# A decoder's sparse experts on one core: a gather waits for the fourth block ahead of it to be turned, in place of the eighth

## Chip, cores and metric

The kernel is one program on one NeuronCore of a Trainium2 chip. TensorE is PE in the views (its weight loads are PEld), VectorE is DVE, ScalarE is ACT, GpSimd is POOL, SyncE is SP. The metric is device time in microseconds, from start to end of one execution; lower is better. All times below are in microseconds unless they say ns.

## What is computed

Twelve sublayers (attention, cross attention and a feed-forward part in each of four layers) run over 1024 tokens of 256 features, each with a residual and a layer norm. The change lies in the last of them, a feed-forward part with 64 experts of which each token uses 8:

```python
logits = x.astype(jnp.float32) @ gate_weight.astype(jnp.float32).T
scores = jax.nn.softmax(logits, axis=-1)
topk_w, topk_idx = jax.lax.top_k(scores, K)          # K = 8 of E = 64
topk_w = topk_w / jnp.sum(topk_w, axis=-1, keepdims=True)
flat_ids = topk_idx.reshape(-1)
sorted_tokens = jnp.repeat(x, K, axis=0)[order]      # order = argsort(flat_ids)
g = jax.lax.ragged_dot(sorted_tokens, w_gate, group_sizes)
u = jax.lax.ragged_dot(sorted_tokens, w_up, group_sizes)
out = jax.lax.ragged_dot(jax.nn.silu(g) * u, w_down, group_sizes)
y = jnp.sum(out[inv].reshape(-1, K, h) * topk_w[:, :, None], axis=1)
```

Each expert has w_gate and w_up of 256x96 and w_down of 96x256. Everything is float32 here.

## The kernel before

The sublayer is `l3_ffn`. A first part (`l3f_route`) sorts the 8192 pairs of token and expert into 127 blocks of 128 places, each block belonging to one expert, and leaves `token_ids` (which token stands in each place) and `experts_row` (which expert each block has). The token rows lie in HBM as `moe_rows`.

The second part (`l3f_experts`) runs over the 127 blocks. Every engine has its own instruction stream, written out by hand, and they meet at semaphores:

- **POOL** (L2544) issues for block b one indirect DMA that gathers 128 rows of 1 KB from `moe_rows` into `rows[:, b % 8, :]`. The buffer is a ring of eight, `x_ring`. Ahead of the gather it waits on `x_turned`, the count of blocks whose rows PE has turned.
- **SP** (L2558) loads the block's expert, 320 KB, into one of six buffers (`w_ring`), once the down product of six blocks earlier is done, and then (L2552) stores the result of that earlier block, 128 KB, to `moe_out`.
- **PE** has, per block, `turn(b)`: wait for the gather, then two transposes (L2571), whose last adds to `x_turned`; `gates(b)`: eight products (L2582), after a wait for the expert's weights; `down(b)`: two instructions in the trace for one product (L2591), after a wait for `h`. The order on PE is turn(b+2), gates(b+1), down(b), for b from 0 on; turn(0), turn(1), gates(0) stand in front.
- **DVE** copies the turned rows from PSUM (L2629) and multiplies silu by the up part (L2657). At block 8, and at blocks 20, 30, ... 90, it also computes a piece of the routing weights (L2634 to L2647).
- **ACT** computes silu (L2611) and copies the down product out of PSUM (L2618).

The wait in front of a gather and what follows it, as they stand in the kernel before:

```python
for b in range(blocks):
    if b >= x_ring:
        pool.wait_ge(x_turned, b - x_ring + 1)
```

The third part (`l3f_combine`) waits on POOL for every store to `moe_out`, gathers eight rows per token from it with 64 indirect DMAs into the same ring `rows`, and DVE sums them (L2679, L2696). It uses `x_ring` for its own waits.

Of the kernel before, what the change touches and what calls it, by code (L numbers as in the profile page):

```python
# [2376 lines left out]
def l3_ffn(k, w):  # L2377
# [6 lines left out]
    numbers, token_past, earlier = w("numbers"), w("token"), w("earlier")  # L2384
    token, past_end = token_past[:, :TILES], token_past[:, TILES:]
    F16 = mybir.dt.float16
    x_ring, w_ring, y_ring = 8, 6, 8
    with ExitStack() as ctx:
        sb = lambda name, shape, dt=F32: k.sb(ctx, "l3f_" + name, shape, dt)
        p, top, tmp = sb("p", [P, TILES, experts]), sb("top", [P, TILES, 8]), sb("tmp", [P, chosen, experts])  # L2390
# [33 lines left out]
        with nc.Block("l3f_route") as block_:  # L2424
# [107 lines left out]
        x_turned, x_copied, gates_done, silu_done, h_done, down_done, y_copied, weighed = (  # L2532
            k.sem("l3f_" + n) for n in names)
# [3 lines left out]
        with nc.Block("l3f_experts") as block_:  # L2537
            @block_.gpsimd
            def _(pool):
                pool.wait_ge(rows_stored, 16)  # L2540
                for b in range(blocks):
                    if b >= x_ring:
                        pool.wait_ge(x_turned, b - x_ring + 1)
                    nc.gpsimd.indirect_dma_start(  # L2544
                        rows[:, b % x_ring, :], None, k.moe_rows,
                        bass.IndirectOffsetOnAxis(token_ids[:, b:b + 1], 0)).then_inc(gathered[b % x_ring], 16)
# [293 lines left out]
```

## Time and profile before

| what | value |
|---|---|
| median of 3 runs | 1949.35 (1949.25 to 1951.55) |
| the profiled execution, its own time | 1946.63 |
| its span, first to last instruction | 1944.8 |
| mean granted TensorE clock | 0.845 of full |
| PE / DVE / ACT / POOL busy, share of the span | 78% / 60% / 43% / 28% |
| DMA moved | 126.19 MB, mean 65 GB/s |

The span is the time between the first and the last instruction of the profiled execution; 1.8 us of its own time lie outside of it. The shares are averages over twelve sublayers with different limits. The change touches the stretch from 1611 us, where the first gather of rows is issued, to about 1845 us, where the combining part starts. So that stretch is read by itself.

### The profile page before, as it was taken

Reading aid. Unit: us, or ns where it says so; the run is one execution under the profiler, and the core shown is the slowest. Engines: PE = TensorE matmul, PEld = TensorE weight load, DVE = VectorE, ACT = ScalarE, POOL = GpSimd, SP = SyncE. Lnnn points to the kernel's source line nnn. Section 1 sums busy time; section 2 is a strip of 40 time slices with the busy share of each in tenths; the row PEclk is TensorE's granted clock in tenths of the full one; section 3 lists DMA queues with packets and bytes.
Section 4 is the critical chain, followed back from the end, with each engine's and each line's share of the span. In section 5 each row is a group of like instructions: output and inputs, shape, how many; then the busy total and the mean of one; then the engine's idle time right before and its main releaser. Section 6 shows DMA issues by size and latency. Waiting matters only on the chain. (4 is left out here: it accounts for less than half of the span.)

```text
span 1944.8 us, 25982 instructions
## 1 busy us (share of the span) xinstructions
PE 1512.2 (78%) x8419; PEld 917.9 (47%) x8419; DVE 1166.2 (60%) x2266; ACT 839.7 (43%) x1649; POOL 554.0 (28%) x578
## 2 busy tenths in 40 slices
PE   5899879986268377768799997899899877999800
PEld 4746635555143122226344445434566456888700
DVE  3537742245755699997999995444366452444343
ACT  2337521122633665634799993211364232333300
POOL 0110100212110599964100001011300415555375
PEclk9999989998679699999655556999999978999955
DMA  2010000010100000001233332000000007999832
GB/s 85 10 61 2 2 22 0 25 57 6 44 30 0 0 1 0 1 1 78 39 74 74 72 71 55 0 1 0 1 2 1 16 22 231 342 347 340 288 108 86
DMA packets 117813, 126.19 MB, mean 65 GB/s; under 512 B 75088, under 2 KB 93648, under 8 KB 116272
## 3 DMA queue, kind: packets, MB, share of 16 engines
q1 hardware_dynamic: 108512, 99.48, 16.7%
q0 software_dynamic: 9168, 25.05, 4.1%
q8 instruction: 69, 1.13, 0.2%
q14 instruction: 64, 0.52, 0.1%
HBM read 88.97 MB, written 18.74 MB: 55 GB/s over the span
## 5 line engine op out<-in xcount | busy, mean ns | idle before, releaser
L446 POOL TENSOR_TENSOR rstd<-var,minus_half 128x1 f32<-128x1 f32 x96 | 61.2, 637 | 724.5 <-DVE var L430 724.5
L1672 POOL TENSOR_TENSOR l_drive<-l_area,l_xpad 128x512 f32<-128x512 f32 x128 | 158.4, 1270 | 88.8 <-ACT l_xpad L1690 88.8
L1646 PE MATMUL psum<-l_drive,consts 128*128 128x512 f32 x256 | 136.1, 635 | 37.8 <-DVE l_drive L1737 37.8
L2069 ACT ACTIVATE l2x_rings<-psum,l2x_mx,l2x_q_s 128x1024 f32<-128x1024 f32 x128 | 154.2, 1205 | 9.0 <-DVE l2x_mx L2040 6.8
L2544 POOL DMA_INDIRECT l3f_rows<-moe_rows,l3f_token_ids x127 | 120.5, 949 | 123.6 <-PE psum L2571 89.4
L2026 DVE TENSOR_REDUCE l2x_mx<-psum 128x1 f32<-128x1024 f32 x128 | 155.1, 1212 | 0.9 <-PE psum L1992 0.9
L1731 DVE TENSOR_TENSOR_SCAN l_state<-psum,l_drive 128x512 f32<-128x512 f32 x128 | 152.1, 1208 | 5.2 <-ACT psum L1703 4.5
L1992 PE MATMUL psum<-l2x_kT,l2x_qT 48*128 48x512 bf16 x256 | 129.9, 612 | 14.4 <-ACT l2x_rings L2069 6.2
L2582 PE MATMUL psum<-l3f_xT,l3f_of_expert 128*96 128x128 f32 x1016 | 134.1, 276 | 0.2
L2629 DVE COPY l3f_xT<-psum 128x256 f32<-128x256 f32 x127 | 53.9, 425 | 133.3 <-PE psum L2571 123.8
L363 ACT ACTIVATE XT<-psum 128x256 f32<-128x256 f32 x88 | 33.8, 384 | 220.1 <-PE psum L398 220.1
L2582 PEld LDWEIGHTS psum<-l3f_xT,l3f_of_expert 128*96 128x96 f32 x1016 | 119.9, 165 | 0.9 <-DMA l3f_of_expert<-in_experts 0.9
L951 DVE TENSOR_REDUCE mx<-psum 128x2 f32<-128x512 f32 (+1 forms) x128 | 79.0, 619 | 54.1 <-PE psum L883 53.5
L1703 ACT ACTIVATE psum<-l_area,l_a_neg 128x510 f32<-128x510 f32 x128 | 87.9, 688 | 46.0 <-DVE l_state L1731 45.7
L2591 PE MATMUL psum<-l3f_of_expert,l3f_h 96*128 96x256 f32 x254 | 88.5, 430 | 14.2 <-DVE l3f_h L2657 8.2
L1646 PEld LDWEIGHTS psum<-l_drive,consts 128*128 128x128 f32 x256 | 44.7, 195 | 104.9 <-DVE l_drive L1737 87.1
L2036 DVE TENSOR_SCALAR l2x_rings<-l2x_rings 128x1024 bf16<-128x1024 f32 x128 | 87.3, 683 | 0.6 <-ACT l2x_rings L2069 0.6
L424 DVE SCALAR_TENSOR_TENSOR R<-X,psum 128x256 f32<-128x256 f32 x80 | 32.7, 409 | 85.6 <-PE psum L387 85.6
L2611 ACT ACTIVATE l3f_silu<-psum 96x128 f32<-96x128 f32 x127 | 34.7, 273 | 103.2 <-PE psum L2582 83.1
L2002 PEld LDWEIGHTS psum<-identity_bf,l2x_rings 128*128 128x128 bf16 x512 | 49.5, 139 | 57.1 <-DVE l2x_rings L2036 57.1
L2679 POOL DMA_INDIRECT l3f_rows<-moe_out,l3f_place_ids x64 | 62.0, 968 | 37.3 <-DMA moe_out<-l3f_y_out 18.8
L2015 PEld LDWEIGHTS psum<-l2x_v,l2x_q_stack 128*128 128x128 bf16 x1024 | 44.9, 111 | 51.9 <-issue 51.0
(473 smaller groups left out, 3272.4 us busy)
## 6 DMA issues: line engine op xcount, KB each, us to landing
l3f_of_expert<-in_experts SPq DMA_DIRECT2D x127, 320.0 KB
moe_out<-l3f_y_out SPq DMA_DIRECT2D x127, 128.0 KB
arena<-in_pack SPq DMA_DIRECT2D x1, 3660.0 KB, 12.3
arena<-in_pack SPq DMA_DIRECT2D x1, 3277.0 KB, 10.3
arena<-in_pack SPq DMA_DIRECT2D x1, 2688.0 KB, 10.1
arena<-in_pack SPq DMA_DIRECT2D x1, 2303.0 KB, 9.0
l3f_rows<-moe_rows,l3f_token_ids POOLq DMA_INDIRECT x127
arena<-in_pack SPq DMA_DIRECT2D x1, 1538.0 KB, 6.7
```

The source lines that it names most:

```text
L951: nc.vector.tensor_reduce(mx[:, p % 4, :], two_heads(p), AX.X, ALU.max, negate=True)\
L1646: nc.tensor.matmul(sum_bank(c), k.identity[:, :], drive[:, (4 * i + c) % 8, :], start=n == 0, stop=n == states - 1, skip_group_check=True) ...
L1672: nc.gpsimd.tensor_tensor(drive[:, (4 * i + c) % 8, :], dx[:, c, half * HALF:(half + 1) * HALF], b_copy[:, i % 2, :], ALU.mult).then_inc(d ...
L1703: nc.scalar.activation(decay_bank(c).rearrange("p (b t) -> p b t", b=2)[:, :, 1:], source[:, :, 1:], ACT.Exp, scale=a_neg[:, c, n:n + 1]). ...
L1731: nc.vector.tensor_tensor_scan(state[:, c, :], decay_bank(c), drive[:, (4 * i + c) % 8, :], 0.0, ALU.mult, ALU.add).then_inc(scanned, 1)
L1992: last = nc.tensor.matmul(score_banks(i)[:, half, :], qT[rows, h // 2, tile * P:(tile + 1) * P], kT[rows, h // 2, half * HALF:(half + 1) * ...
L2026: nc.vector.tensor_reduce(mx[:, i % 4, 0:1], score_banks(i), AX.XY, ALU.max, negate=True).then_inc(max_taken, 1)
L2036: nc.vector.tensor_scalar(whole[:, u % 4, :], e[:, u % 3, :], ROUND, -ROUND, ALU.add, ALU.add).then_inc(rounded, 1)
L2069: nc.scalar.activation(e[:, i % 3, :], score_banks(i).rearrange("p b t -> p (b t)"), ACT.Exp, bias=mx[:, i % 4, 1:2], scale=q_s[:, i:i + 1 ...
L2544: nc.gpsimd.indirect_dma_start(rows[:, b % x_ring, :], None, k.moe_rows, bass.IndirectOffsetOnAxis(token_ids[:, b:b + 1], 0)).then_inc(gat ...
L2582: last = nc.tensor.matmul(k.bank(2 + b % 2)[:inter, n * P:(n + 1) * P], wgu[:, b % w_ring, c, n * inter:(n + 1) * inter], xT[:, b % 3, c, ...
L2591: nc.tensor.matmul(k.bank(4 + b % 2)[:, :D], h[:inter, b % 2, :], wd[:inter, b % w_ring, :], start=True, stop=True, skip_group_check=True) ...
```

## The change

The wait in front of the gather for block b asks for another count. Before, it was passed once PE had turned block b-8, which is also when the buffer that the gather writes comes free. Now it is passed once PE has turned block b-4. The ring keeps its eight buffers, and the gather still writes `rows[:, b % 8, :]`. Blocks 4 to 7 get a wait that they did not have. Nothing else differs; the combining part keeps its waits by `x_ring`.

```diff
-    x_ring, w_ring, y_ring = 8, 6, 8
+    x_ring, w_ring, y_ring, ahead = 8, 6, 8, 4
@@
                 for b in range(blocks):
-                    if b >= x_ring:
-                        pool.wait_ge(x_turned, b - x_ring + 1)
+                    if b >= ahead:
+                        pool.wait_ge(x_turned, b - ahead + 1)
                     nc.gpsimd.indirect_dma_start(
                         rows[:, b % x_ring, :], None, k.moe_rows,
                         bass.IndirectOffsetOnAxis(token_ids[:, b:b + 1], 0)).then_inc(gathered[b % x_ring], 16)
```

## Rows read from the trace of the kernel before

**Rows 1.** Busy time by stretch: us, engines, granted clock, DMA share, GB/s.
```profile
core 0: us, PE busy (x) PEld busy (x) DVE busy (x) ACT busy (x) POOL busy (x), PEclk, DMA share, GB/s
1611.00:1636.00 25.00, 15.37 (x88) 13.70 (x89) 4.54 (x14) 4.23 (x14) 15.40 (x16) 0.75 0.76 233
1636.00:1838.00 202.00, 192.87 (x1413) 173.44 (x1411) 90.56 (x264) 77.01 (x235) 105.06 (x111) 1.00 0.99 339
1838.00:1845.00 7.00, 4.61 (x28) 3.22 (x26) 1.18 (x4) 2.36 (x7) 0.00 (x0) 1.00 0.39 136
```

**Rows 2.** Waits, 1636 to 1838: who waits for whom, total us, times, longest.
```profile
POOL l3f_rows L2544 <- PE psum L2571: 85.9, 109, 2.2
...
PEld psum L2591 <- DVE l3f_h L2657: 9.9, 9, 1.4
...
PEld psum L2582 <- DMA l3f_of_expert<-in_experts: 0.4, 1, 0.4
```

**Rows 3.** Timeline of PE's weight loads: start, us, engine, line, operation.
```profile
1820.46 0.36 PEld L2571 LDWEIGHTS psum<-consts,l3f_rows 128*128 128x128 f32 x2
...
1822.09 0.36 PEld L2571 LDWEIGHTS psum<-consts,l3f_rows 128*128 128x128 f32 x2
...
1826.97 0.36 PEld L2571 LDWEIGHTS psum<-consts,l3f_rows 128*128 128x128 f32 x2
```

**Rows 4.** Timeline of POOL at the end of the blocks.
```profile
1821.34 0.94 POOL L2544 DMA_INDIRECT l3f_rows<-moe_rows,l3f_token_ids  x1 [0.69 <-PE psum L2571]
...
1826.22 0.94 POOL L2544 DMA_INDIRECT l3f_rows<-moe_rows,l3f_token_ids  x1 [0.68 <-PE psum L2571]
1845.91 0.94 POOL L2679 DMA_INDIRECT l3f_rows<-moe_out,l3f_place_ids  x1 [18.75 <-DMA moe_out<-l3f_y_out]
```

**Rows 5.** Timeline of the first gathers and of the first turn.
```profile
1610.96 1.22 POOL L2544 DMA_INDIRECT l3f_rows<-moe_rows,l3f_token_ids  x1 [27.92 <-POOLq L2424]
...
1612.48 0.95 POOL L2544 DMA_INDIRECT l3f_rows<-moe_rows,l3f_token_ids  x1 [0.30 <-issue]
...
1615.14 0.29 PEld L2571 LDWEIGHTS psum<-consts,l3f_rows 128*128 128x128 f32 x2 [6.42 <-DMA l3f_rows<-moe_rows,l3f_token_ids]
```

**Rows 6.** Timeline of POOL around one of DVE's extra pieces.
```profile
1662.01 0.95 POOL L2544 DMA_INDIRECT l3f_rows<-moe_rows,l3f_token_ids  x1 [0.68 <-PE psum L2571]
1664.71 0.95 POOL L2544 DMA_INDIRECT l3f_rows<-moe_rows,l3f_token_ids  x1 [1.75 <-PE psum L2571]
```

**Rows 7.** DMA queues, 1666.9 to 1667.2: packets, MB, share; q0 carries gathers.
```profile
q1 hardware_dynamic: 65, 0.12, 104.1%
q0 software_dynamic: 2, 0.00, 3.5%
```

**Rows 8.** DMA queues, 1667.2 to 1667.43, every queue that moved anything.
```profile
q1 hardware_dynamic: 52, 0.09, 97.5%
```

**Rows 9.** DMA queues, 1830 to 1830.5; in the next half microsecond q0 has none.
```profile
q1 hardware_dynamic: 110, 0.17, 94.3%
q0 software_dynamic: 5, 0.01, 4.3%
```

**Rows 10.** Timeline of PE near the start of the blocks.
```profile
1620.94 1.04 PE L2582 MATMUL psum<-l3f_xT,l3f_of_expert 128*96 128x128 f32 x8
1624.43 0.70 PE L2591 MATMUL psum<-l3f_of_expert,l3f_h 96*128 96x256 f32 x2 [2.45 <-issue]
...
1628.77 0.70 PE L2591 MATMUL psum<-l3f_of_expert,l3f_h 96*128 96x256 f32 x2 [2.55 <-issue]
```

**Rows 11.** The chain that ended last, 1830 to 1846: start, us, what.
```profile
1834.85 5.55 DMA l3f_of_expert<-in_experts
...
1840.44 1.13 PE psum L2582 x8
...
1843.38 1.68 DMA moe_out<-l3f_y_out
```

## The prediction, made before the changed kernel ran

> **What bounds the kernel now.** I read the busy time by stretch first, since the page's shares average over twelve sublayers. From 1636 to 1838 us PE is busy 192.87 of 202 us at the full granted clock (1.00, its 2.4 GHz level), and the DMA engines are busy for a share of 0.99 [rows 1]. So PE sets the pace and the transfers are nearly full beside it. The waits of the same stretch say who is late: POOL waits for PE 109 times in front of a gather, PE waits for DVE's `h` nine times (9.9 us), and PE waits for a DMA once, 0.4 us, for weights. It never waits for gathered rows there [rows 2]. Then the timeline gives the beat: turns begin at 1820.46, 1822.09 and, four blocks after the first, at 1826.97, so a block takes 6.51 / 4 = 1.63 us [rows 3]. POOL issues a gather 0.88 us after the start of the turn that releases it (1821.34 - 1820.46) [rows 3, 4].
>
> **What the change does to a gather.** The same turn still releases a gather, at the same place in the beat, but it is now the gather for the block four turns later. Before, it had eight blocks less 0.88 us, 13.01 - 0.88 = 12.1 us, to land. Now the gather issued at 1821.34 would be for the turn at 1826.97: 5.63 us [rows 3, 4]. No instruction is added in the steady part; the four new waits (blocks 4 to 7) are of a kind POOL passes 119 times already.
>
> What does a gather take, from its issue to its last packet, in this traffic? The gathers follow each other so closely on their queue (q0) that the last packet of one can be told only where a pause follows. The one issued at 1662.01 is followed by one at 1664.71 [rows 6]; q0 has two packets from 1666.9 to 1667.2 and none from there to 1667.43 [rows 7, 8]. So it ended 4.9 to 5.2 us after its issue. The last one, issued at 1826.22, has its last packets between 1830 and 1830.5, 3.8 to 4.3 us after [rows 4, 9]. The very first, beside the first loads of weights, was issued at 1610.96 and let PE start at 1615.14, 4.2 us [rows 5]. All three lie under 5.63 us, by 0.4 to 1.8 us. The typical gather is in time; the margin is thin, where before it was over 6.9 us.
>
> A rule speaks for a wider margin. The Trainium skill ("DMA: Bandwidth & Descriptors", Anatomy of one DMA) fits a DMA issued from GpSimd as about 2.0 us plus bytes over 436 GB/s. By that, an estimate for 128 KB is 2.3 us; no gather could be late, and the time would stay where it is. The rows above show 3.8 to 5.2 us at a DMA share of 0.99, so they decide here; the same page (Latency and other measured facts) says that HBM's latency is several times larger at high load, in which direction the trace agrees.
>
> **The price, part by part.**
>
> 1. Late gathers in the steady part. A turn that waits stops PE, and since PE sets the pace, the whole wait is lost: behind the turn on PE stand gates(b-1) and down(b-2), and behind them silu, `h`, the copy, the store and the next load. From below this costs 0, if the 111 gathers of the stretch behave like the three seen. From above: a large transfer in this traffic, a load of weights, took 5.55 us [rows 11]; no row shows one of a gather above 5.2. But 16 engines must finish for one gather, two of the three measured ones stood next to a pause or the end, and the three spread over more than a microsecond, so some of the 111 will pass 5.63. I take one in ten late by 0.2 us: 11 x 0.2 = 2.2 us. Upper bound for the likeliest case: one in ten by 0.4, 4.4 us.
>
> 2. The start. Gathers 4 and 5 are not held: POOL needs 1.25 us for each and comes to gather 4 at about 1616, when the first turn (1615.14) is done. Gathers 6 to 11 go out later than before, up to one every turn. PE is itself slow there: 1.9 to 4 us per block at a mean granted clock of 0.75 and with two gaps [rows 1, 10]. So each has more than 5.63 us. Cost 0.
>
> 3. DVE's extra pieces. Each holds PE for 2.70 - 1.63 = 1.07 us [rows 6], nine times in all. They hold turn and gather alike; a gather that spans one has 6.7 us. Cost 0, and a late gather may hide here.
>
> 4. The end. Four gathers more are in the air while the last weights come in: the last is issued near 1826.22 + 6.5 = 1832.7. The load issued at 1834.85 lands after 5.55 us, and the chain goes from its landing to PE at 1840.44, so nothing covers it [rows 11]. About half a gather to two (64 to 256 KB at the stretch's 339 GB/s, 0.2 to 0.75 us) may come in front of it. I take 0.4 us; the bounds are 0 and 0.75. POOL has nothing else to do: it next waits for the stores until 1845.91 [rows 4], so its own later last gather costs nothing there.
>
> 5. What is saved. No work goes. SP, ACT and DVE have the same instructions, in the same order. The gathers' bytes are the same and their place in the beat too, so the DMA share stays at 0.99; only the burst at the start is thinner.
>
> The sum is 2.2 + 0.4 = 2.6 us. The profiled execution took 1946.63 us, 1.8 of them outside its span, so its like would come to 1949.2. The three timed runs lie higher, with a median of 1949.35 and a spread of 2.3 us; on that median the forecast is **1952.0 us**, in a range of its own from 1949.3 (nothing late) to 1954.5 (4.4 + 0.75).
>
> **The rivals.**
>
> *The gather loop binds (slower).* A turn releases a gather after 0.88 us and that gather releases the turn four blocks on, so no block can be shorter than (0.88 + landing) / 4. At 5.2 us that is 1.52, under PE's 1.63; it decides from 5.63 us on. If the gathers in the middle of the stretch, which the trace does not separate, take 5.9 us on average, the beat is 1.695, and 0.067 x 120 blocks = 8 us. One in four late by 0.3 us gives the same: 28 x 0.3 = 8.4. That is 1957.5. For it: the DMA share of 0.99, and that 5.2 was seen right behind a pause. Against it: a slower beat also thins the traffic, and weights, which are larger, arrive within their own 5.6 us or so. Chance 0.36 with everything that costs over 3.9 us.
>
> *The start gets shorter (faster).* PE stands still for 2.45 and 2.55 us near 1622 and 1626 [rows 10], with POOL issuing gathers back to back meanwhile. Should these gaps come from POOL's gathers being in the way of the others, holding gathers 7 to 11 back would shrink them, by at most 5.0 us: 1949.35 - 5.0 + 0.4 = 1944.8. Against it: the stretch's DMA share is 0.76, not full, PE's gap is put down to no transfer, and the same gathers run beside PE without gaps later. Chance 0.07.
>
> *The wait never matters.* If every gather lands within 5.63 us and the last weights have room, nothing moves: 1949.35. It lies inside the forecast's own range, with about a third of its chance.
>
> **How the numbers follow.** About 0.2% (3.9 us) is what a measurement of this kernel can tell from no change. The forecast, with the case of no cost at all, has 0.57; the slower loop 0.36; the shorter start 0.07. The forecast of 2.6 us lies within 0.2%. Range: 1947.5 to 1960. It leaves out most of the shorter start and a loop with landings above 6 us.
>
> **What would show each step.** Right: the turns (L2571) wait for the gather's DMA a few to a dozen times, some 2 us in all; the idle of POOL in front of L2544 hardly changes in total; the last gather is issued near 1833; the beat between is still 1.63 us. Wrong: a beat above 1.65 between late gathers (the loop binds), or the gaps at 1622 and 1626 gone. If the turns never wait, step 1 is 0 and any loss must sit at the last load. What would upset it most is a tail of slow gathers longer than the three seen.

## The result and the profile after

| | before | after |
|---|---|---|
| median | 1951.49 | 1947.14 |
| profiled execution, its span | 1944.8 | 1945.6 |
| first gather of rows to first gather of the combining part | 234.95 | 230.46 |

The ratio of after to before is 0.9977, with an interval of 0.9969 to 0.9984. So the change makes the kernel 0.23% faster, 4.5 us, where I forecast a loss of 2.6 us; the time also lies just under my range.

The two spans alone would say the opposite. In the profiled execution of after, the first gather of rows goes out at 1615.18, in that of before at 1610.96. These 4.2 us arise ahead of the code that was changed, and the combining part, which is the same code, takes 100.0 us in after and 98.8 in before. In four of the profiled executions below, and in some timed runs of either kernel, the part ahead of the stage ran some 30 us longer, and the ratios are of timed runs without that; in all other profiles the first gather goes out between 1608 and 1616 us. So I read the stage from its first gather on. There after needs 4.5 us less, as the timed runs say.

PE's timeline at the start of the blocks, after (start, us, engine, line, operation, idle before it):

```profile
1625.57 0.60 PE L2591 MATMUL psum<-l3f_of_expert,l3f_h 96*128 96x256 f32 x2
1626.01 0.38 PE L2571 MATMUL psum<-consts,l3f_rows 128*128 128x128 f32 x2
1626.23 1.04 PE L2582 MATMUL psum<-l3f_xT,l3f_of_expert 128*96 128x128 f32 x8
1627.10 0.70 PE L2591 MATMUL psum<-l3f_of_expert,l3f_h 96*128 96x256 f32 x2
...
1634.13 0.38 PE L2571 MATMUL psum<-consts,l3f_rows 128*128 128x128 f32 x2
```

The gaps of 2.45 and 2.55 us of [rows 10] are gone: PE goes from turn to turn at 1.63 us a block from the fourth turn on. The last line is the turn of block 8, 18.95 us after the first gather. Before it was at 1635.66, 24.7 us after. POOL's timeline after, at the start and at the end:

```profile
1620.45 0.95 POOL L2544 DMA_INDIRECT l3f_rows<-moe_rows,l3f_token_ids  x1 [0.30 <-issue]
1622.90 0.94 POOL L2544 DMA_INDIRECT l3f_rows<-moe_rows,l3f_token_ids  x1 [1.50 <-PE psum L2571]
1625.03 0.94 POOL L2544 DMA_INDIRECT l3f_rows<-moe_rows,l3f_token_ids  x1 [1.19 <-PE psum L2571]
...
1832.50 0.94 POOL L2544 DMA_INDIRECT l3f_rows<-moe_rows,l3f_token_ids  x1 [0.68 <-PE psum L2571]
1845.64 0.94 POOL L2679 DMA_INDIRECT l3f_rows<-moe_out,l3f_place_ids  x1 [12.20 <-DMA moe_out<-l3f_y_out]
```

Five gathers go out back to back, then each follows a turn; before, twelve went out 1.25 us apart. The last is issued 13.1 us ahead of the first combining gather, where it was 19.7 in [rows 4]. Behind the start there is a price, in the waits of after from 1636 to 1838 us (who, for whom, us, times, longest), which answer to [rows 2], and in its chain:

```profile
POOL l3f_rows L2544 <- PE psum L2571: 89.4, 112, 2.2
...
PEld psum L2571 <- DMA l3f_rows<-moe_rows,l3f_token_ids: 1.5, 2, 1.1
```

```profile
1830.87 6.02 DMA l3f_rows<-moe_rows,l3f_token_ids
...
1836.94 0.44 PE psum L2571 x2
```

PE's turns now wait for gathers. The gather issued at 1830.87 took 6.02 us, over the 5.63 us it has. It stands in the chain, and the load of weights of [rows 11] does not. From the turn of block 16 to that of block 126 the two profiles have 188.6 us before and 190.2 after, 1.6 more. So 5.7 us are gained up to block 8, 1.6 lost behind it, and 0.3 gained at the end. Only the first of these is clear of scatter: in the five profiles of the kernel before that this study has, the stretch from turn 16 to turn 126 takes 188.6 to 190.2 us.

### The profile page after: what moved, and what is told of

Its sections match the earlier page's. It is cut to its first block and busy times, and to the rows that moved or that the text cites. A ratio compares the mean times of both kernels' runs of the same rounds, so it can differ in the third digit from the quotient of the medians.

```text
span 1945.6 us, 25980 instructions
## 1 busy us (share of the span) xinstructions
PE 1514.7 (78%) x8417; PEld 919.6 (47%) x8419; DVE 1166.5 (60%) x2266; ACT 839.0 (43%) x1649; POOL 553.9 (28%) x578
```

## The experiments

My theory after the result, A: POOL's gathers, issued back to back at the start, make PE late; holding them back removes the gaps. Rivals: the gain comes from the steady part (B), or the gaps come and go whatever the kernel (C). The chip of a run turned out to matter, so this table comes first; it has every profile. "Back to back" is how many gathers POOL issued 1.25 us apart from the first on; "turn 8" is the time from the first gather of rows to the start of block 8's turn, both from the timelines; "combining" is the time from the first combining gather to the end.

| chip | kernel (blocks ahead) | back to back | turn 8 | combining |
|---|---|---|---|---|
| not named | before (8) | 12 | 24.7 | 98.8 |
| not named | after (4) | 5 | 18.9 | 100.0 |
| 1 | before again (8) | 11 | 24.2 | 98.9 |
| 1 | 8 up to block 15, then 4 | 11 | 24.2 | 98.9 |
| 1 | 4 up to block 15, then 8 | 5 | 18.8 | 98.9 |
| 1 | 3 | 3 | 18.8 | 98.9 |
| 2 | 5 / 6 / gradual | 8 / 11 / 5 | 18.2 / 18.6 / 18.9 | 93.0 |
| 2 | 4, with five stretches of 5 to 8 | 6 | 18.4 | 92.9 |
| 3 | 7 | 16 | 18.3 | 93.1 |
| 3 | 5, with extra gathers, thin / full | 20 / 18 | 19.7 / 20.7 | 93.0 / 93.1 |
| 3 | 4 up to block 15, then 8, again | 5 | 18.6 | 92.9 |
| 4 | before twice (8) | 11 and 11 | 25.0 and 26.2 | 99.8, 100.0 |
| 4 | after again (4) | 6 | 18.4 | 99.9 |
| 4 | 7 | 10 | 23.5 | 100.1 |
| 5 | before (8) | 11 | 25.0 | 99.7 |
| 5 | 5, with extra thin gathers | 12 | 27.0 | 99.7 |

On one named chip the combining part varies by 0.3 us at most. The first two profiles differ by 1.1 us there, so they may come from two chips. The gain of the stage does not hang on that pair: on chip 4 it shows again, below.

**The first half of the change alone**

```diff
-                    if b >= ahead:
-                        pool.wait_ge(x_turned, b - ahead + 1)
+                    lead = 4 if b < 16 else 8
+                    if b >= lead:
+                        pool.wait_ge(x_turned, b - lead + 1)
```

> Gathers of blocks 4 to 15 wait for the block four places ahead, all later ones for the block eight ahead, as before. Theory A (the gain of the change lies in its first 15 blocks, where the gathers held back leave PE's results in time): the whole gain and none of the late gathers, 4 to 6 us under the kernel before, the gaps of PE near the start gone, and no wait of a turn for a gather after the first blocks. Theory B (the gain lies in the steady part, through thinner traffic): within 1 us of the kernel before. Theory C (the gaps at the start come and go between executions whatever the kernel): within 1 us of the kernel before, with the gaps in some profiles.

The gaps at the start are gone (18.8 us), so B falls. The ratio of the timed runs is 1.001 (0.998 to 1.004), which tells nothing: the runs of either kernel scatter over 6 us on this chip. The profile has the stage at 232.96 us, 1.9 less than the kernel before on the same chip, and not the 5 of theory A, because a gap of another place has come. PE's timeline (the lines of this kernel are one higher):

```profile
1673.19 0.38 PE L2572 MATMUL psum<-consts,l3f_rows 128*128 128x128 f32 x2
1676.37 0.70 PE L2592 MATMUL psum<-l3f_of_expert,l3f_h 96*128 96x256 f32 x2 [1.92 <-issue]
...
1680.07 0.70 PE L2592 MATMUL psum<-l3f_of_expert,l3f_h 96*128 96x256 f32 x2 [1.91 <-issue]
```

and ACT's:

```profile
1673.56 0.27 ACT L2612 ACTIVATE l3f_silu<-psum 96x128 f32<-96x128 f32 x1 [1.42 <-PE psum L2583]
1674.99 0.38 ACT L2619 ACTIVATE l3f_y_out<-psum 128x256 f32<-128x256 f32 x1 [1.15 <-remote]
1679.32 0.27 ACT L2612 ACTIVATE l3f_silu<-psum 96x128 f32<-96x128 f32 x1 [3.94 <-PE psum L2583]
```

From block 16 on the kernel lets gathers go for a block eight ahead, and POOL issues seven back to back, from 1669.29 on. In that time PE's products reach ACT late: the gates that PE begins at 1673.41 are used by ACT at 1679.32. The same shows before the change at 1622 and 1628. So the gap is in the middle of the stage here, at full clock, where the crowd of gathers is.

**The second half alone**, with `lead = 8 if b < 16 else 4`:

> The other half: blocks up to 15 as before the change, later gathers wait for the block four ahead. Theory A: no gain, 0 to 2 us slower than the kernel before (some late gathers, the gaps at the start stay). Theory B: the gain of the change, about 4 us. Theory C: as the kernel before.

Turn 8 is at 24.2 us, PE stands near the start for 1.25 and 1.92 us, and the late gathers are there too: 190.9 us from turn 16 to turn 126, where the kernel before on this chip has 189.4. The stage takes 236.7 us, 1.8 more than before (timed: 1.0001, 0.9968 to 1.0033). The steady part of the change is no gain, and by this pair of profiles a small loss. The kernel before once more, on the same chip:

> The kernel before once more, for a second profile of its start. Theory A: PE again has two gaps of about 2.5 us in the first blocks, before the product of down. Theory C: this profile may well have none, and the same stretch is then about 5 us shorter.

The place is the expected one, the form is not: PE stands once, for 2.17 us, and its granted clock is 0.50 from 1615.0 to 1623.1 and 0.53 from 1626.4 to 1630.0. Turn 8 is 5.4 us later than in the first half alone, so the idle time is under half of the loss, and slow products are in the rest. Part of the low clock lies ahead of the gap, and no run says why. So far theory A held for the place and the sum.

**Three ahead**, with `lead = 3`:

> Every gather waits for the block three ahead, which measures what a gather takes in the traffic. A turn releases a gather after 0.88 us and may itself start when that has landed, so a block takes (0.88 + landing) / 3. With landings of 4.6 to 5.2 us that is 1.83 to 2.03 us against PE's 1.63, over about 120 blocks 24 to 48 us slower. If gathers land in under 4 us when there is no crowd on their queue, it costs nothing and keeps the gain of about 4 us.

The waits of the stretch from 1631 to 1861 us:

```profile
PEld psum L2572 <- DMA l3f_rows<-moe_rows,l3f_token_ids: 37.1, 43, 2.7
```

A block takes 216.05 / 110 = 1.96 us from turn 16 to turn 126. If about one turn in three waits, as 43 of 118 do in these rows, then (0.88 + landing) / 3 makes a landing of 5.0 us, as an estimate; the turns that came late began 5.1 us (median) after the issue of their gather. The stage is 26.8 us longer than in the profile of after and 22.3 longer than the kernel before on this chip, the time 1.0105 of before (1.0034 to 1.0176). So the law of the gather loop, one of my rivals, describes three ahead. With a landing of 5.0 us four ahead gives 1.47 us, under PE's 1.63; so it does not bind the changed kernel.

**Crowds of growing length in the steady part**: four ahead, but for ten blocks each from block 29, 49, 69, 89 and 109 on five, six, seven, eight and eight.

```diff
+                    lead = {29: 5, 49: 6, 69: 7, 89: 8, 109: 8}.get(...)   # first block of the stretch: lead in it
```

> Gathers wait for the block four ahead, but in five stretches of ten blocks for a block farther ahead: from block 29 for the one 5 ahead, from 49 for 6, from 69 for 7, from 89 and from 109 for 8. At the head of each stretch POOL has 1, 2, 3, 4 and 4 gathers more to issue, and issues 2, 3, 4 and 5 or more back to back. Theory A (a crowd of gathers back to back makes PE's results late, at the start or not): no gap for the first one or two stretches, gaps of 2 to 4 us of PE at the last three, growing with the number, after turns 67, 87 and 107 or so. Theory D (the start is special: the clock rises, the weights of six blocks arrive): no gap at any of them, as the clock is full and six buffers of weights are under way at all times.

No gap at any of the five, though POOL issues 5, 9, 11, 11 and 11 gathers back to back at their heads: no turn in them comes over 0.2 us late but for DVE's pauses. Theory A seemed to fall, as it did with the next ones:

> Gathers up to block 15 wait for the block 4 ahead, from 16 for 5, from 24 for 6, from 32 for 7, from 40 for 8 ahead: at no place more than one extra gather at a time. Theory A: the start as in the changed kernel (turn of block 8 about 18.9 us after the first gather, in place of 24 to 25), no gaps later, no late gathers after block 16; the stage of the blocks 5.5 to 6 us shorter than before and 1 us shorter than with the change, 1 us or so more than that where the gaps of the first 15-block kernel were. Theory D: the same start; but the single extra gathers cost nothing under it either, so this run tells only whether both gains can be had.

> Every gather waits for the block five ahead: 5 x 1.63 - 0.88 = 7.25 us to land. Theory A: no late gather, and at the start one gather more back to back than with the change; if the gaps need a crowd of more than six, the stage is 5.5 us shorter than before; in time about 5 us under the kernel before, 1 us under the change. If the change's late gathers cost nothing, it is as fast as the change.

> Every gather waits for the block six ahead. Theory A: no late gathers; at the start six or seven gathers go out back to back. If the crowd decides by its length, part of the gap of PE at the start is back: turn of block 8 between 19 and 24 us after the first gather. If a gap needs the twelve of the kernel before, it is at 19.

None has a gap, and none is measurably faster than the kernel before: five ahead 1.0003 (0.9993 to 1.0012), gradual 0.998 (0.9949 to 1.0011). The first of these two is the telling one. It is a tight interval, on this chip, around no difference, for a start that on the first chips was worth 0.2%.

**Extra gathers near the start**, in the kernel with five ahead:

```diff
+                    if 4 <= b < 8:
+                        nc.gpsimd.indirect_dma_start(
+                            y[:, b - 4, :D], None, k.moe_rows,
+                            bass.IndirectOffsetOnAxis(token_ids[:, b:b + 1], 0)).then_inc(extra, 16)
```

> The kernel with the block five ahead, with four gathers more: behind each of the gathers of blocks 4 to 7 POOL issues another gather of 128 rows of 1 KB into a buffer that nothing uses (work added, the result is the same). At the start POOL then issues about ten gathers back to back, as before the change, while no block's own gather goes out earlier. Theory A (it is the crowd of gathers near the start): the gaps of PE are back, turn of block 8 about 24 us after the first gather in place of 18.2. Theory F (it is something else of the kernel before, such as the second use of the ring): it stays at 18 to 19.

> The same with four extra gathers of 64 bytes a row: nearly the same work for POOL (issue and descriptors), a sixteenth of the bytes. If the gaps come from POOL's work they are there as with the full ones (24 us); if from the transfers they are gone (18 to 19 us).

Again no gap of that kind. The 1.5 to 2.5 us over 18.2 are turns that wait for their own gathers, which POOL now issues later (2.9 and 2.2 us in their waits). Together with these:

> Every gather waits for the block seven ahead. With 6 the turn of block 8 stood 18.6 us after the first gather, with 8 at 24.2 to 24.7. Theory A in steps: 7 lies between or at one of the two, which gives the threshold; below 19.5 the gaps need the full ring of eight.

Seven ahead issued 16 gathers in a row and has turn 8 at 18.3 us. The first experiment, repeated here, has no gap after turn 13 either, though POOL issues 14 gathers in a row from block 16 on:

> The first experiment once more (4 ahead up to block 15, then 8), for a second profile of its gap after turn 13. If the gap belongs to the kernel it is there again: turns 13 to 15 take 3.7 us each in place of 1.63. If it was chance, the turns take 1.63.

Two readings were left: the gaps come and go (C), or chips 2 and 3 have none whatever the kernel, and then these profiles say nothing against A. The combining part, which is the same code everywhere, takes 93 us on these two and 99 to 100 us on the others, so the chips do differ in how gathers go.

**The same kernels on one more chip**

> The kernel before, on the chip of the next three kernels. Theory P (eight ahead leaves PE with the gaps whatever the chip): turn of block 8 about 24 to 25 us after the first gather, as in three profiles so far. Theory C (the gaps come and go between executions or chips; a kernel with seven ahead had none although its first 16 gathers went out back to back): about 18.5 us in this profile or the next.

> The kernel before again, as the one ahead. Theory P: 24 to 25 us. Theory C: where one of the two has gaps and the other none, they come and go on one chip; where both have none, the chip may decide.

> The changed kernel against the one before on this chip. Theory P: 4 to 5 us faster, as in the first measurement. Theory C: as fast as the kernel before where the two profiles ahead have no gaps, that is 0 to 2 us slower by the late gathers.

> Seven ahead, timed. At the start it issues its gathers as the kernel before does, in the first 15 us within a fraction of a microsecond. Theory P (a threshold between seven and eight): 5 us faster than the kernel before. Theory C: no difference to the kernel before beyond 1 us.

On this chip the kernel before has its gap in both profiles, seven ahead has it too, and four ahead has not. PE in the second profile of the kernel before, then in seven ahead:

```profile
1623.19 1.04 PE L2582 MATMUL psum<-l3f_xT,l3f_of_expert 128*96 128x128 f32 x8
1629.35 1.22 PE L2591 MATMUL psum<-l3f_of_expert,l3f_h 96*128 96x256 f32 x2 [5.12 <-DVE l3f_h L2657]
```

```profile
1654.37 1.04 PE L2582 MATMUL psum<-l3f_xT,l3f_of_expert 128*96 128x128 f32 x8
1658.81 0.70 PE L2591 MATMUL psum<-l3f_of_expert,l3f_h 96*128 96x256 f32 x2 [3.40 <-DVE l3f_h L2657]
```

The changed kernel is at 0.9958 of before (0.9943 to 0.9973), seven ahead at 0.999 (0.998 to 1.000). The gain is there again. Its size, 8 us by four runs of the changed kernel, is more than the 3.4 and 4.8 us by which its stage is shorter than in the two profiles of the kernel before. Two of the four runs are 7.0 and 9.5 us faster than the profiled one, and no profile shows where. So seven ahead is no threshold: it has the gap on chip 4 and none on chip 3, with the same start.

**One chip more**

> The kernel before, one look. So far five ahead, six ahead, seven ahead and the extra gathers had no gap on two chips, and seven ahead has one on a third, where eight ahead has it twice. Theory G (a crowd of gathers makes the gaps, on some chips only; those also take about 99 us for the combining part in place of 93): with a combining part of about 93 us the turn of block 8 stands at about 18.5 us, with one of about 99 us at 24 to 26 us. Theory P (eight ahead has gaps on every chip): 24 to 26 us either way.

> Five ahead with four extra gathers of 64 bytes a row behind those of blocks 4 to 7, again. It tells something only where the kernel before has gaps on this chip. If the gaps come from POOL's issuing and the descriptors they are there, 22 us or later for the turn of block 8; if from the gathered bytes, it stands at 19 to 20 us, as on the chip where nothing had gaps.

Chip 5 has a combining part of 99.7 us and the gap. POOL and PE in the kernel with thin extra gathers (L2549 is the extra one):

```profile
1622.21 0.95 POOL L2549 DMA_INDIRECT l3f_y<-moe_rows,l3f_token_ids  x1 [0.30 <-issue]
1623.46 0.95 POOL L2545 DMA_INDIRECT l3f_rows<-moe_rows,l3f_token_ids  x1 [0.30 <-issue]
1624.71 0.94 POOL L2549 DMA_INDIRECT l3f_y<-moe_rows,l3f_token_ids  x1 [0.30 <-issue]
1627.99 0.94 POOL L2545 DMA_INDIRECT l3f_rows<-moe_rows,l3f_token_ids  x1 [2.34 <-remote]
```

```profile
1620.89 1.04 PE L2587 MATMUL psum<-l3f_xT,l3f_of_expert 128*96 128x128 f32 x8
1628.43 1.22 PE L2596 MATMUL psum<-l3f_of_expert,l3f_h 96*128 96x256 f32 x2 [6.51 <-issue]
```

A gather of 64 bytes a row takes POOL as long (0.95 us) as one of 1 KB. With four of them in the row, PE stands for 6.51 us, the longest gap of all, though the gathered bytes are fewer than in the kernel before. The DMA share is 0.81 from 1610.7 to 1621 and 0.36 from 1621 to 1628.4, while PE stands. So it is not the gathered bytes. It is POOL issuing gathers back to back, or what comes with one whatever its size.

**A place that nearly every kernel has**

In every kernel but the one with five stretches, POOL's gathers of blocks 112 and 113 (120 and 121 where extra gathers were added) are issued 3.1 us apart, and POOL then catches up; what makes the pause is not shown. The changed kernel there:

```profile
1811.41 0.95 POOL L2544 DMA_INDIRECT l3f_rows<-moe_rows,l3f_token_ids  x1 [2.16 <-PE psum L2571]
1812.66 0.95 POOL L2544 DMA_INDIRECT l3f_rows<-moe_rows,l3f_token_ids  x1 [0.30 <-issue]
1813.61 0.69 PE L2591 MATMUL psum<-l3f_of_expert,l3f_h 96*128 96x256 f32 x2
1813.91 0.95 POOL L2544 DMA_INDIRECT l3f_rows<-moe_rows,l3f_token_ids  x1 [0.30 <-issue]
1815.93 0.37 ACT L2618 ACTIVATE l3f_y_out<-psum 128x256 f32<-128x256 f32 x1
1816.51 0.70 PE L2591 MATMUL psum<-l3f_of_expert,l3f_h 96*128 96x256 f32 x2 [1.11 <-issue]
```

ACT copies the down product 1.62 us after its end, where 0.04 us is usual, and PE stands for 1.11 us. So it is in all twelve profiles with a combining part of 99 to 100 us, whether three or eight ahead: three gathers 1.25 us apart, and ACT's copy 1.05 to 1.65 us late. In the seven profiles of 93 us with the same pause, three or five gathers go out 1.25 us apart and the copy is 0.04 us behind its product. So on the first chips a run of three is enough for a short gap, in the changed kernel too. The pause ahead of the run, or what made it, is not told apart from the run here.

What the runs show together: on the three named chips with a combining part of 99 to 100 us, each of the seven profiles in which POOL issues ten or more gathers back to back at the start has a gap there, and the first experiment has none there but one where it issues seven in a row from block 16. The other two profiles (three ahead, and four ahead on chip 4) have no such crowd and no gap at the start. On the two chips with 93 us, none of eight profiles has a gap, with crowds of up to 11 on chip 2 and 20 on chip 3 or without.

What stays open: whether the kernel before has no gap on the chips of 93 us. It was never profiled there; seven ahead, which issues as it does, and the timing of five ahead against it speak for that. So does an estimate: on chip 2 its timed runs have a median of 1937.1 us; less 1.8 outside the span, 93.0 for the combining part and a first gather at 1611 to 1615, that leaves 227 to 231 us for the stage, near the 227.8 of five ahead there and under the 235 with a gap.

Open is also how POOL's issuing holds up PE's results. The form of the trace is that PE's products are listed on time and used by ACT, DVE and POOL 2 to 6.7 us late. In the profile of before the first down product is listed until 1620.9; the rise of its semaphore is recorded at 1623.69, and ACT and SP go on at 1623.71. Whether the product or only its semaphore is late the trace does not say, since the ends of products are modelled.

One rival was not tested: the recording itself. The traces of the chips of 93 us hold 127 rises of the semaphore of `h`, one for each block, and some 8500 rises by DMAs; those of the others hold 22 to 31 and 4300 to 5200. So on the chips with gaps the trace loses records of semaphores, and whether the recording also delays the semaphores is not shown. And five ahead was not tried on a chip with gaps, so the changed kernel is the best that was measured there.

## Why the prediction was wrong

*The steady part was right in cause and about right in size, which was in part luck.* I put the late gathers at 2.2 us, as one in ten late by 0.2 us. The stretch is longer by 1.6 us in the profile of after, by 1.6 in the second half alone (190.9 against 189.4 on its chip), and by 3.2 in the second profile of after, on chip 4 (192.0 against 188.8), with a scatter of 1.6 in the kernel before. PE's weight loads for the turns wait for rows twice in the profile of after, 1.5 us in all; in the second half alone four times, 2.7 us, and on chip 4 three times, 2.4 us (PE itself stands for 0.7, 1.1 and 1.1 us of it). So fewer gathers are late than I said, each by more, up to 1.2 us. The budget of 5.63 us and the loop of (0.88 + landing) / n fit. The usual landing, 5.0 by the loop, lies where I put it; the late ones let their turns start 5.9 to 6.7 us after the issue, beyond the 0.2 to 0.4 us that I allowed over 5.63. The trace also agrees with what I said against the fit of the Trainium skill ("DMA: Bandwidth & Descriptors", Anatomy of one DMA): landings are more than twice the 2.3 us estimated from it in this traffic, and three ahead, which by that fit would cost nothing (3 x 1.63 - 0.88 = 4.0 us), lost 27 us of stage.

*The end was slightly off.* I put 0.4 us there, and no loss shows. The time from the last turn to the combining part is 7.0 us after and 7.0 to 7.3 in the five profiles of the kernel before.

*The step that failed is the second, the start, at cost 0.* I checked whether gathers held back would still be in time, which they are, and took PE's gaps there as given. (That gather 5 is not held was wrong too: it waits for a turn, 1.50 us in the rows above.) In place of 0 the start gains 5.7 us up to block 8, because with POOL's gathers held back PE's products reach the other engines in time. The saving stood among the rivals with the right place, cause and size ("by at most 5.0 us") and a chance of 0.07. The three reasons that I gave against it do not hold. The DMA share of 0.76 was no evidence, since bytes are not the cause; the longest gap came with thin gathers. "PE's gap is put down to no transfer" pointed the same way: it said that the cause was not a transfer, and what was left was POOL, which issued through the first gap and up to 1625.96, just ahead of the second, and then stood waiting itself. And "the same gathers run beside PE without gaps later" was wrong in "the same": later each follows a turn, 1.63 us apart, and at the start they go 1.25 us apart with no wait between. Where they once go 1.25 us apart later, at 1805 to 1808 in the profile of before, PE does have a gap, of 0.99 us at 1810.39.

There was a further sign in the rows of before. After the two gaps PE's granted clock fell below full. The busy time of before by stretch (columns as in [rows 1]), and its timeline:

```profile
1630.00:1634.00 4.00, 4.00 (x20) 3.65 (x19) 0.96 (x4) 0.86 (x3) 1.86 (x2) 0.57 0.93 265
1634.00:1640.00 6.00, 6.00 (x47) 5.47 (x46) 2.51 (x9) 2.43 (x8) 3.28 (x4) 1.00 0.92 295
```

```profile
1630.64 1.06 PE L2591 MATMUL psum<-l3f_of_expert,l3f_h 96*128 96x256 f32 x2
1631.49 0.63 PE L2571 MATMUL psum<-consts,l3f_rows 128*128 128x128 f32 x2
1631.92 1.84 PE L2582 MATMUL psum<-l3f_xT,l3f_of_expert 128*96 128x128 f32 x8
...
1635.66 0.38 PE L2571 MATMUL psum<-consts,l3f_rows 128*128 128x128 f32 x2
1635.88 1.04 PE L2582 MATMUL psum<-l3f_xT,l3f_of_expert 128*96 128x128 f32 x8
```

From 1630 to 1634 the granted clock is 0.57, near the lower level of 1.2 GHz, and then full. In it the gates take 1.84 us for 1.04, the turn 0.63 for 0.38. So a gap of PE can cost more than its own length. My bound of 5.0 us for the two gaps was exceeded, with 5.7 us gained up to block 8, and on chip 1 a single gap of 2.17 us goes with a loss of 5.4; that the clock is the whole of these differences was not shown.

## What to carry to other kernels

A wait that holds an engine back can be a gain: a deep ring lets POOL run ahead of need, and what it takes from the others by that is paid at once, while the depth is needed only later. Where an engine stands in a gap that no transfer and no engine explains, list what ran in it or just ahead of it and treat it as a suspect with a real chance. And look at a stage by itself, on more than one chip, before a difference of 0.2% is believed or given up.

## What was not expected of the hardware

- POOL takes 0.95 us to issue a gather of 128 rows, of 1 KB or of 64 bytes alike, and 1.25 us from one to the next.
- On some chips a run of seven to twelve such issues makes PE's results 2 to 6.7 us late and stops PE for 2 to 6.5 us in a row, and a run of three behind a pause makes them 1.1 to 1.7 us late; on two other chips runs of three to 20 did nothing.
- After such a gap PE's granted clock can be low for some microseconds (0.57 over 4 us before), and the products in that time take about 1.7 times as long (1.84 us for 1.04).
- The chips where this happens need 99 to 100 us for 64 gathers from `moe_out` and what follows them; the others need 93.
